# Relation stage of a graph network: a relation's matrix fetched in six pieces over two chunks instead of in two halves at once

## The reference

```python
seg = edge_type * n + dst
agg = jax.ops.segment_sum(x[src], seg, num_segments=N_REL * n)
cnt = jax.ops.segment_sum(ones, seg, num_segments=N_REL * n)
mean = agg.reshape(N_REL, n, -1) / jnp.maximum(cnt, 1.0).reshape(N_REL, n, 1)
h1 = jnp.einsum('rni,rio->no', mean, W_rel) + x @ W_root + b_rgcn
```

## Time and profile before

| | us |
|---|---|
| median of three timed runs | 2891.39 |
| profiled execution, its own time | 2897.0 |
| its span, first to last instruction | 2895.3 |
| TensorE busy (83% of the span) | 2415.6 |
| VectorE busy (52%) | 1511.7 |
| ScalarE busy (37%) | 1064.2 |
| GpSimd busy (33%) | 950.8 |
| mean granted TensorE clock, share of full speed | 0.92 |

### The profile page before, as it was taken

One profiled execution on the slowest core, in us unless ns is written; L12 is line 12 of the kernel. 1 busy time (PEld: TensorE's weight loads), 2 busy tenths in 40 slices (PEclk: granted clock), 3 DMA queues, 4 the chain that ended last, 5 costly groups with the idle time before them and its releaser, 6 DMA issues.

```text
span 2895.3 us, 49957 instructions
## 1 busy us (share of the span) xinstructions
PE 2415.6 (83%) x13014; PEld 2249.7 (78%) x13015; DVE 1511.7 (52%) x2625; ACT 1064.2 (37%) x1833; POOL 950.8 (33%) x1172
## 2 busy tenths in 40 slices
PE   3777579867899988889999997788878879977799
PEld 1455579767888888888888887566777879977799
DVE  6655574643333433333333334777745687687534
ACT  3212322223333333333333333555522245446421
POOL 4666001134444444444444444777700000000000
PEclk9999899989889999988999998789989989989899
DMA  6000103544444454444444444877711110011102
GB/s 209 1 0 0 50 6 140 189 174 153 158 157 163 166 176 163 158 163 152 160 156 163 172 170 154 247 224 222 235 71 52 69 38 0 11 44 54 55 11 97
DMA packets 117614, 346.41 MB, mean 120 GB/s; under 512 B 28615, under 2 KB 29595, under 8 KB 117509
## 3 DMA queue, kind: packets, MB, share of 16 engines
q1 hardware_dynamic: 73045, 205.21, 19.4%
q0 software_dynamic: 44528, 140.69, 15.7%
HBM read 258.18 MB, written 91.47 MB: 121 GB/s over the span
## 4 chain that ended last, share of the span: by engine, by line
PE 63%; DVE 11%; issue 8%; another core or an unknown queue 6%; ACT 5%; DMA 4%; DVEq 2%; POOL 1%; ACTq 0%; POOLq 0%; SPq 0%
PE ps L1525 41%; PE ps L1582 11%; PE ps L1516 5%; PE ps L1652 4%; DMA land<-messages,stage 2%; PE ps L1726 1%; DVE h_act L1108 1%; ACT land L854 1%; DVE xw L1482 1%; DVE w_a L1031 1%; DVE land L1167 1%; DVE land L1427 1%; ACT agg_w L824 1%; DVE land L1121 1%
## 5 line engine op out<-in xcount | busy, mean ns | idle before, releaser
L1525 PE MATMUL ps<-w_a,h_t 128*128 128x384 f32 x4968 | 944.2, 347 | 17.8 <-issue 15.2
L1525 PEld LDWEIGHTS ps<-w_a,h_t 128*128 128x128 f32 x4968 | 895.2, 196 | 27.8 <-issue 23.8
L1582 PE MATMUL ps<-xw,agg_w 128*128 128x384 f32 x2800 | 536.2, 354 | 109.4 <-DVE agg_w L1130 71.8
L1582 PEld LDWEIGHTS ps<-xw,agg_w 128*128 128x128 f32 x2800 | 521.2, 200 | 121.6 <-issue 109.7
L1431 DVE TENSOR_TENSOR h_t<-ps,h_t 128x256 fp32r<-128x256 f32 x408 | 169.8, 423 | 713.8 <-ACT h_t L962 629.5
L1525 PE MATMUL ps<-xw,h_t 128*128 128x384 f32 x2448 | 481.9, 355 | 8.0 <-issue 7.8
L1525 PEld LDWEIGHTS ps<-xw,h_t 128*128 128x128 f32 x2448 | 455.2, 199 | 10.5 <-issue 9.9
L962 ACT ACTIVATE h_t<-ps 128x256 fp32r<-128x256 f32 x408 | 153.2, 383 | 751.4 <-PE ps L1525 385.4
L674 POOL DMA_INDIRECT h_act<-h_table,stage x139 | 147.1, 1058 | 517.3 <-DVE land L1427 493.4
L1516 PE MATMUL ps<-ident,land 128*128 128x128 f32 x1176 | 183.7, 298 | 154.0 <-DVE land L1427 104.1
L1516 PEld LDWEIGHTS ps<-ident,land 128*128 128x128 f32 x1176 | 152.5, 154 | 175.9 <-DVE h_t L1431 116.5
(11 more groups left out here) (224 smaller groups left out, 2122.8 us busy)
## 6 DMA issues: line engine op xcount, KB each, us to landing
land<-in_L_gnn_W_rel SPq DMA_DIRECT2D x68, 1152.0 KB
messages<-land SPq DMA_DIRECT2D x136, 384.0 KB
land<-x_state SPq DMA_DIRECT2D x40, 384.0 KB, 3.1
messages<-land POOLq DMA_DIRECT2D x34, 384.0 KB, 2.6
land<-in_L_gnn_W SPq DMA_DIRECT2D x10, 1152.0 KB
x_state<-land SPq DMA_DIRECT2D x30, 384.0 KB, 2.3
adj<-x_state SPq DMA_DIRECT2D x10, 384.0 KB
h_act<-x_state SPq DMA_DIRECT2D x1, 3840.0 KB
```

Of the source, the lines that this page charges most:

```text
L1525: ins = pe.matmul(acc(h), h_t[:, a, k, :], w[:, b, k, h * HF:(h + 1) * HF], start=(k == 0 and a == 0 and b == 0), stop=(stop and k == KB - ...
L1582: ins = pe.matmul(ps[:, 2 + 2 * u + h, 0:wide], agg_w[:, a, b, :], xw[:, c, b, h * HF:h * HF + wide], start=first, stop=last, skip_group_c ...
```

## The change

The change is in SyncE's stream, and in the counts that ScalarE waits for. `next_matrix` becomes `next_half`. A half goes out as three DMAs of one block (128x768, 384 KB) each; the second waits for the landing of the first, and the third for that of the second. Nobody waits for the landing of the third on SyncE. The first half follows the store of the relation's first chunk, as before. The second waits for `yout` to reach c0+4, that is for `rel_out` of the second chunk, and then goes out in the same manner. Both stand ahead of the second chunk's store. The matrix of relation 1, which was fetched before the stage began, now also waits for the first gather to have landed (`R.ready`).

```diff
-            def next_matrix(r, w):
-                for h in range(2):
-                    sp.wait_ge(w_low, r * 2 + (w_no["rel"] * 2 - 1 + h))
-                    sp.dma_start(w_raw[:, 3 * h:3 * h + 3, :],
-                                 w[:, 3 * h * P:3 * (h + 1) * P, :].rearrange("a (k p) d -> p (a k) d", p=P))\
+            def next_half(r, w, h):
+                sp.wait_ge(w_low, r * 2 + (w_no["rel"] * 2 - 1 + h))
+                for k in range(3):
+                    if k > 0:
+                        sp.wait_ge(w_land[h], r * 48 + (w_no["rel"] * 16 - 32 + k * 16))
+                    sp.sem_inc(turn_taken, 1)
+                    b = 3 * h + k
+                    sp.dma_start(w_raw[:, b:b + 1, :], w[:, b * P:(b + 1) * P, :].rearrange("a (k p) d -> p (a k) d", p=P))\
                       .then_inc(w_land[h], 16)
...
                 store(c0, c0, base)
                 if w is not None:
-                    next_matrix(r + 2, w)
+                    next_half(r + 2, w, 0)
+                    sp.wait_ge(R.yout, c0 + 4)
+                    sp.sem_inc(turn_taken, 1)
+                    next_half(r + 2, w, 1)
                 with sp.Fori(c0 + 1, c1) as c:
                     store(c, c0, base)
             sp.wait_ge(K.dve, K.ctl)
-            next_matrix(1, w_rel[1:2, :, :])
+            sp.wait_ge(R.ready, 1)
+            for h in range(2):
+                next_half(1, w_rel[1:2, :, :], h)
...
-                    act.wait_ge(w_land[h], n * 16 + 16)
+                    act.wait_ge(w_land[h], n * 16 + 16 + (32 * NR if n > w_no["rel"] else 0))
...
-                    act.wait_ge(w_land[p // 3], r * 16 + (w_no["rel"] * 16 + 16))
+                    act.wait_ge(w_land[p // 3], r * 48 + (w_no["rel"] * 16 + 16))
```

## The result

The changed kernel takes 2939.65 us, the median of 4 runs (2926.23 to 2947.19); the kernel before, timed beside it, 2890.97 (2885.45 to 2898.07). The ratio is 1.0138, 95% interval 1.0106 to 1.0171: the change costs 49 us. That lies in the range of 2808 to 2942, 2 us inside its upper end, but the likeliest case was no change at 2894, and that is missed by 46 us. What came is the rival "SyncE's chain becomes the bound" (chance 0.18, priced at 2960).

A forecast was written before the change was run, and what follows sets the result against it. TensorE's matmuls fill 28.1 of each relation's 33.9 us; late semaphores and a slower clock were to remain. Profiled 2897.0, 33 relations x 0, start +3: 2900, or 2894 on the runs' scale; range 2808 to 2942.

The forecast's parts named there:

- SyncE's chain becomes the bound: Fourth chunk's rel_out waits for the second chunk's store, from 4.0 us a landing; 2960 at 4.5 us; chance 0.18.
- The late semaphore: TensorE's semaphore reaches ScalarE late, 148.8 us in total; blamed on GpSimd's lookups, not the load; effect 0.
- the sign of being wrong that was named: ScalarE's "remote" waits falling below 50 us would show that the matrix load caused them.
- the rival "faster": The load causes the late semaphores; relations fall until SyncE's chain stops them at 30.5 us; 2782 or 2840; chance 0.27.
- SyncE's chain: SyncE's stores and waited landings, 3.1 us each, level with the old schedule by the fourth chunk's store; effect 0.
- The slack: Second chunk's store was to land 3.7 us before the fourth chunk's rel_out needs it.
- TensorE's waits, and line 956: TensorE's waits before its turns stay near 92 us; the copy-out of rel_out never waits for a store.
- The condition named for being wrong: Waits for SyncE at line 956, the copy-out of rel_out, would show that the chain lags.
- The first matrix: At the stage's start, first gather 2.6 us sooner but second half later: +3 us, between -3 and +9.
- Counts: ScalarE's changed semaphore numbers and SyncE's six counter steps: under 0.1 us each, in the slack.
- the rule alone: Skill's DMA rules: a piece takes 2.9 us, 2 of them fixed; six cost 12 us a relation instead of 4.

The follow-up runs named there:

- e6_after_again: The changed kernel, unchanged, run again on another chip beside the kernel before: 2903.9 us, ratio 1.08.
- e5_before_again: The kernel before, unchanged, run again for its trace on another chip: 2681.99 us, ratio 0.9979.
- e3_pieces_unwaited: The changed kernel without SyncE's waits for landings, each half three DMAs back to back, on another chip: 2684.13 us, ratio 0.9996 to the kernel before.

## Why the prediction missed

**The late semaphore: it stayed, and its cause is open.** No effect of the change on it was forecast, with ScalarE's "remote" waits near 149 us. They are 192.9 us, in 39 waits instead of 22, so the sign of being wrong that was named (below 50 us) did not come, but "near 149" did not hold either. No more than 768 KB of the matrix are queued at once now. So the whole matrix in one go is not their cause, and the rival "faster" did not come. ScalarE and GpSimd in the trace of after still show the pattern of the earlier trace rows:

```profile
1082.46 0.66 ACT L970 ACTIVATE h_t<-ps 128x256 fp32r<-128x256 f32 x2 [8.17 <-remote]
```

```profile
1079.93 0.95 POOL L693 DMA_INDIRECT stage<-inv_table,stage  x1 [0.30 <-issue]
1084.94 0.95 POOL L682 DMA_INDIRECT h_act<-h_table,stage  x1 [4.06 <-DVE land L1435]
```

The release comes 1.6 us after the train of lookups ends (1082.46 less 1080.88; 1.7 before). But on the other chips the same trains run and no wait for "remote" is there. None of the eleven runs there has one. The train is at most one of the conditions; my sentence that the late semaphore "belongs to the lookups" claims more than one chip could show.

**SyncE's chain: this is the step that failed.** "Effect 0" rested on SyncE being level with its old schedule at the end of the relation. The rival "faster" had the chain's length at 30.5 us; it is 35.5 in the trace of after and 34.4 in `e6_after_again`. By term, in means over 30 relations of each:

| step | forecast | after | `e6_after_again` |
|---|---|---|---|
| first store to first piece | 2.63 | 4.17 | 2.97 |
| piece to piece, four times | 3.3, 3.3, 4.2, 3.3 | 3.48, 3.75, 3.47, 3.93 | 3.91, 3.49, 4.65, 3.89 |
| between halves; last piece to second store | 0.7; 1.1 | 2.04; 1.04 | 0.81; 1.06 |
| second store to third | 3.1 | 4.27 | 4.93 |
| the other two stores and the head of the next relation | 8.95 | 9.33 | 8.64 |

On the first chip, where the forecast was made, it was not the waited landings. From issue to landing a piece took 3.3 us on average, as forecast, and the four steps between pieces are 14.6 us instead of 14.1. The sum failed in the steps around them, which it had taken over from the old schedule. The first three stores landed in 3.4, 3.4 and 3.1 us where the sum had 2.3 to 2.7: 1.5 us more before the first piece, 1.2 more between second and third store. Between the halves another 1.3 us went. Part of the chain of waits in after, there:

```profile
1044.42 0.68 SPq L547
1045.12 0.69 issue
1045.84 0.70 issue
1046.61 0.34 SPq L547
```

The second chunk's `rel_out`, for which SyncE looks here, had ended at 1038.09. So SyncE waits for no data that is still being made: the issue of a piece takes 0.68 us instead of 0.34, and 0.7 us stand between instructions that follow each other in less than 0.1 in `e6_after_again` (there 0.81 from piece to piece, here 2.19). There are 50 pauses of more than 0.4 us before an instruction that waits for nothing in these 31 relations, and none in the traces of the changed kernel and its variants on other chips. 40 of the 50 fall in a train of at least six of GpSimd's indirect DMAs, or less than 2.5 us behind one, which is 39% of the time. The late semaphores are seen at such trains as well. I can't say what causes either.

On the other chips these pauses are absent, and two other terms carry 3.7 of the 3.8 us. The waited landings took 3.8 us on average, the four steps 15.9 us: the 3.1 came from transfers of x_state, which take 3.0 there, and not from this stage. And the sentence "The second chunk's store at 1026.9, landed 2.3 us to 2.7 later": nobody waits for the last piece, so the store is issued 1.1 us behind it in the same queue and lands in 4.0 on average, where the last store of a relation takes 2.3. I had given the piece that starts 0.7 us behind another 0.9 us for its company, and the store in nearly the same position 0.4 at most.

**The slack.** It was measured as 3.7 us at one place of one relation in which TensorE lost 6 us to a late semaphore. By the table, the second store on the first chip has landed 1.5 + 0.5 + 1.3 - 0.1 + 0.7 = 4.0 us later than forecast (3.35 for 2.7 in the last term), and the 3.7 are gone. ScalarE is idle before the fourth chunk's `rel_out` for 2.7 us on average in after, and not at all before the change. On that chip the lateness, which the relation of 33.9 us already held, covered most of the longer stream: 35.5 against 33.9, 1.6 us x 31 relations. Where it is absent, 34.5 stand against 28.0. (The experiments ran there; for the first chip the cause rests on the two traces: the slack of 11.3 us gone, and the waits of the fourth chunk's `rel_out`.)

**What was luck.** The rival asked for landings of 4.0 us and more, and was priced at 4.5. It came with landings of 3.3. Its place and its mechanism were right, and its price (2960 for 2939.65) was near, but through other terms than those it was worked out from. That the time lies inside the range is due to the width that this rival asked for, and to relations that were already long on the first chip: where they are 28 us the same change costs 217 us and not 49.

**TensorE's waits, and line 956.** They were to stay near 92 and are 147.2 us: the chain shows up in them. The condition named for being wrong, waits of the copy-out for SyncE, is met (43.9 us in 17 waits, and 174.4 in 25 in `e6_after_again`), and at the place named: every idle time of more than 1 us before a `rel_out` is at the fourth chunk's, 32 in after and 33 in `e6_after_again`.

**The first matrix.** +3 us was forecast, as a gain of 2.6 at the first gather and a loss behind it. The first gather, and VectorE's copy of it, in the trace of after:

```profile
614.40 1.02 POOL L682 DMA_INDIRECT h_act<-h_table,stage  x1 [0.66 <-POOL stage L678]
...
618.31 0.56 DVE L1451 COPY land<-h_act 128x768 f32<-128x768 f32 x1 [8.97 <-POOLq L707]
```

From issue to copy it is 3.91 us, where the earlier trace rows have 6.51: the gain of 2.6 came. (6.54 and 4.07 in `e5_before_again` and `e6_after_again`.) The gather itself is issued 5.87 us later than before, ahead of anything that the change touches; the other runs issue it between 605.9 and 611.4. From its issue to the start of the 31 relations after has 86.81 us (to 701.21) and before 90.07 (608.53 to 698.60), so the start is 3.3 us shorter, not 3 longer; the loss does not show on this chip. In the pair on the other chip it is 9.8 us longer (76.97 for 67.17), of which two relations at 34.5 us instead of 28.0 would be 13 (an estimate), so the loss of the first matrix is not separated from the chain there.

**Counts, and the size of a piece.** The added counter steps were put at nothing, and `e3_pieces_unwaited` bears that out. The Trainium skill, "DMA: Bandwidth & Descriptors", section "Anatomy of one DMA", has about 2 us of fixed time on a transfer. It gives this figure for transfers that GpSimd issues. The pieces are SyncE's, and an 8 KB piece takes 1.8 to 2.5 us there from issue to landing, so this case agrees. The section "Rules for kernel authors" asks for at least 1 MiB per DMA where full bandwidth is wanted. From the two I had concluded that the kernel would lose by the rule alone. It did lose, but the size of the pieces did not do it: six pieces of 384 KB cost nothing until somebody waits for each.

## What to carry to other kernels

A wait for a landing on an engine that also issues stores is a term of a sum: write down that engine's whole stream, landings and all, and set it against the floor of the bound engine (28.0 us here), not against a period that contains stalls of another cause. Read its slack in the profile before the change: it is the time that the engine waits for the data of others. If the cycle is within a few microseconds of it, price each transfer by what is ahead of it in its own queue; a store behind an unwaited 384 KB piece landed in 4.0 us instead of 2.3. In the trace of after, look whether that engine still waits for data: when it waits only for its own transfers, it is the bound, whatever the busy shares say.

## What the runs showed of the hardware that was not expected

The same kernel took 2891 us on one chip and 2683 to 2687 on three others. 186 of the 213 us between the spans of its two traces lie in the 31 relations (1051.30 and 864.98), 23 in the first two. On the first chip ScalarE waits up to 8 us for "remote", TensorE stops, and the granted clock over the 31 relations is 0.91; on the other the clock is 1.00. In the changed kernel SyncE's own instructions stand 0.7 us apart in places there. What differs between the chips is not shown.

A stop of TensorE cost more than its idle time: after 3.77 us of it the next twelve matmuls took 3.81 us instead of 2.2, at a granted clock of 0.58.
